# Preparing and finishing the node rows inside the edge loop of a graph attention layer

## The chip, the core and the metric

The program runs on 1 core of one Trainium2 chip. The metric is the device time of one execution in microseconds. A core has TensorE (PE in the rows, with its weight loads as PEld), VectorE (DVE), ScalarE (ACT), GpSimd (POOL) and SyncE (SP). Each works through its own list of instructions in order, and they meet at semaphores. Copies between HBM and the memory on the core go through 16 DMA engines; they are issued by SP or ACT, or, for the gathers with an index per row, by GpSimd.

## What is computed

```python
h = jnp.maximum(_layernorm(x, axis=-1), 0.0)      # x: 6250 nodes x 256
eq = h @ Wq + bq
ek = h @ Wk + bk
e = edge_attr @ We + be                            # 106250 edges x 256
m = jax.nn.relu(eq[dst] + ek[src] + e)
ft = jax.ops.segment_sum(m, dst, num_segments=6250)
return x + (ft @ Wr + br)
```

The edges come sorted by dst, and there are 17 of them per node on average (each of 50000 drawn pairs both ways, and one loop per node).

## The kernel before

Every float32 product is made of three float32r products: each operand is split into a rounded part (hi, made by ScalarE) and the rest (lo, made by VectorE), and hi·hi, hi·lo and lo·hi are added up in PSUM (`split_product`, the matmuls of line 934, whichever product it is).

**Node phase.** Nodes lie in 52 blocks of 128. SP loads x into the space that later holds `ft` (four loads), VectorE takes row statistics (line 688), GpSimd works out variance, scale and shift in three parts (lines 441 to 459). Then per block: ScalarE makes h (`make_h`, line 534), TensorE transposes it (943), ScalarE and VectorE split the transpose (541, 709), TensorE makes k and q side by side (6 matmuls of 512 columns), VectorE adds the biases from PSUM into `kq` (717), ScalarE rounds q (547), GpSimd makes q's low part (465), and SP stores the k rows in `k_table` and both q parts in `q_table` in HBM (`store_tables`, lines 305 and 310). Side work (the windows of the groups, weights of the edges, clearing `ft`, line 733) is spread over these turns.

**Edge loop.** 208 groups of 512 edges, four to a body, so 52 bodies. A group's destinations lie in a window of 48 nodes. For group n, in this order on each engine:
- GpSimd: four gathers of 128 k rows by src (`gather`, line 494) into one of four slots, once the slot's group n-4 was added (`s_pre`).
- VectorE, one step per group: `add_rows` (838: adds the gathered rows to the edge product in PSUM; it waits until the gathers of group n+1 have been written too, `s_wrote`), `make_send` (826), `add_sum` (862: adds the sum of group n-3 to `ft`), `edge_low` (818: low part of the edges of group n+2), `message_low` (846).
- ScalarE: `copy_idx` (586), `edge_high` of n+2 (594), `message_high` (615), `make_pick` of n+2 (604, 607), `take_sum` of n-1 (622).
- TensorE: `edge_product` of n+1 (28 matmuls, lines 934 and 989: the edge product and, by a one-hot matrix, the q rows of the window), `window_sum` of n-1 (8 matmuls, 1012), `turn_part` of n-2 (2 transposes, 999). The edge product of n+1 goes into the PSUM slot of n-1, so it waits for `message_low` of n-1.
- SP: loads of edges, window indices and q windows for the group four ahead.

The order that matters for VectorE and TensorE:

```python
for u in range(UNROLL):                    # VectorE
    add_rows(it, u, last)
    make_send(it, u)
    add_sum(it, u - 3, w0)
    edge_low(it, u + 2)
    message_low(it, u)
for u in range(UNROLL):                    # TensorE
    edge_product(it, u + 1)
    window_sum(it, u - 1)
    turn_part(it, u - 2)
```

**Output phase.** After the last sum, per block of `ft`: ScalarE and VectorE split it (655, 896), TensorE makes the product with Wr (6 matmuls), VectorE adds x+br, which GpSimd has prepared (512), two blocks at a time (908), and SP stores four blocks at a time (399).

All edges are done in one pass if every group's destinations fit into 48 nodes; otherwise the program repeats the loop over all windows (`more_passes`, `passes_of`).

Of the kernel before, what the change touches and what calls it, by code (L numbers as in the profile page):

```python
# [22 lines left out]
LANES = 128  # L23
NODES = 6250
# [22 lines left out]
TURNS = BLOCKS // NRING  # L47
NORM_STEPS = (None, 0, 17)
STATS_STEPS = NORM_STEPS[2]
SIDE_TURNS = 6  # L50
PAIRS = NRING // 2
X_SLOTS = 8
OUT_SLOTS = 4
LOAD_TURNS = SIDE_TURNS + UNROLL
LEAD = 2
assert TURNS % OUT_SLOTS == 1 and OUT_SLOTS == TILES and UNROLL == OUT_SLOTS and X_SLOTS == UNROLL + 4
assert BLOCKS % NRING == 0 and BLOCKS % 2 == 0 and 2 * NRING * (TURNS - SIDE_TURNS) >= BLOCKS and BLOCKS % XPARTS == 0
# [3 lines left out]
def gnn_program(nc, x, dst_groups, dst_lanes, src_lanes, edges, Wq, bq, Wk, bk, We, be, Wr, br, out):  # L61
# [5 lines left out]
    k_table = nc.dram_tensor("k_table", (ROWS, D), F32, kind="Internal").ap()  # L67
    q_table = nc.dram_tensor("q_table", (2, ROWS, D), F32R, kind="Internal").ap()
# [9 lines left out]
    with ctx:  # L78
# [12 lines left out]
        lane_raw = sb("lane_raw", [2 * WIN, PASSES], F32)  # L91
        lane_wrap = sb("lane_wrap", [2 * WIN, 1], F32)
        lane_node = sb("lane_node", [2 * WIN, PASSES], F32)
        lane_id = sb("lane_id", [2 * WIN, 1], F32)
# [9 lines left out]
        span = sb("span", [LANES, 1], F32)  # L104
        narrow = sb("narrow", [LANES, 1], F32)
# [11 lines left out]
        bias = sb("bias", [LANES, 2 * D], F32)  # L117
        bias_e = sb("bias_e", [LANES, D], F32)
        bias_r = sb("bias_r", [LANES, D], F32)
# [22 lines left out]
        gap = sb("gap", [2 * WIN, GROUP], I16)  # L142
# [7 lines left out]
        x_slots = [edge[:, u].rearrange("p h e -> p (h e)") for u in range(UNROLL)]  # L150
        slot_cols = 2 * NRING * D
        x_slots += [window_cols[:, u * slot_cols:(u + 1) * slot_cols].bitcast(F32) for u in range(3)]
        x_slots += [pre[:, 0, :]]
        x_slots = [slot.rearrange("p (b d) -> p b d", d=D) for slot in x_slots]
        result = k_rows

        kq = k_rows[:, 0:2].rearrange("p s t d -> p (s t d)").rearrange("p (b n) -> p b n", n=2 * D)
# [7 lines left out]
        sum_rows = sb("sum_rows", [LANES, 2, D], F32)  # L165

# [74 lines left out]
        def stored(eng, stores, b, u):  # L241

            if isinstance(b, int) and b < NRING:
                return
            eng.wait_ge(stores[u], 16 // NRING * (b - u))
# [850 lines left out]
```

## Time and profile before

| | us |
|---|---|
| median of 3 runs | 1247.06 (1246.17 to 1247.19) |
| the profiled execution's own time | 1248.51 |
| its span in the profile | 1246.6 |
| TensorE busy | 1119.9 (90%) |
| VectorE busy | 962.8 (77%) |
| ScalarE busy | 857.2 (69%) |
| GpSimd busy | 887.7 (71%) |
| DMA | 303.48 MB, mean 243 GB/s |

The span runs from the first to the last instruction in the profile. Busy time counts the instructions that compute (and GpSimd's writing of gather descriptors). Matmuls overlap in the array, so a busy TensorE need not be a full one. "Idle before" is the time for which an engine stood still before instructions of a group, and the name behind the arrow is what it was released by.

### The profile page before, as it was taken

The numbers are of one execution on the slowest core, as the hardware profiler recorded it, in microseconds if no ns is written. First come the engines' busy times: TensorE is split into PE (matmuls) and PEld (weight loads), VectorE is DVE, ScalarE is ACT, GpSimd is POOL, SyncE is SP. The second block draws the span as 40 slices with busy tenths as digits, with TensorE's granted clock in tenths as the row PEclk, the third lists the DMA queues.
The fourth block names the chain that finished last, engine by engine and source line by source line (L and its number), as shares of the span: only waits on it lengthen the run. The fifth ranks groups of instructions, "written<-read, shape, count | busy, mean of one in ns | idle before, by whom it ended". The sixth has DMA issues, their size and how long they took to land.

```text
span 1246.6 us, 33342 instructions
## 1 busy us (share of the span) xinstructions
PE 1119.9 (90%) x8632; PEld 1051.0 (84%) x8632; DVE 962.8 (77%) x1324; ACT 857.2 (69%) x1463; POOL 887.7 (71%) x946
## 2 busy tenths in 40 slices
PE   1997799999999999999999999999999999999876
PEld 1775789889898888898898988888988989898875
DVE  5887577777777777777777777777777777777798
ACT  1676577777777777777777777777777777777542
POOL 4454777777777777777777777777777777777644
PEclk9999999999999999999999999999999999999989
DMA  8888777777778777777777777777877787877664
GB/s 249 273 275 273 237 244 246 245 244 243 254 246 248 245 246 247 250 248 244 244 245 251 244 252 245 244 247 247 251 246 245 245 248 242 256 244 244 209 191 140
DMA packets 164469, 303.48 MB, mean 243 GB/s; under 512 B 29204, under 2 KB 110740, under 8 KB 164452
## 3 DMA queue, kind: packets, MB, share of 16 engines
q1 hardware_dynamic: 124516, 194.18, 50.0%
q0 software_dynamic: 39936, 109.11, 27.0%
q8 instruction: 6, 0.10, 0.0%
q14 instruction: 11, 0.09, 0.0%
HBM read 275.69 MB, written 27.48 MB: 243 GB/s over the span
## 4 chain that ended last, share of the span: by engine, by line
POOL 46%; issue 37%; PE 9%; DVE 3%; DMA 3%; ACT 1%; POOLq 1%; SPq 0%; DVEq 0%; ACTq 0%
POOL k_rows L494 46%; PE p_sum L934 5%; PE p_edge L934 3%; DVE hT_lo L896 1%; DMA ft<-in_x 1%; PE p_turn L943 1%; DMA k_rows<-k_table,idx 1%; POOLq L502 0%; DMA pre<-in_dst_groups 0%; DMA range_table<-top_g 0%; DVE k_rows L908 0%; DVE k_rows L717 0%; POOLq L492 0%; DVE p_edge L838 0%; ACT hT_hi L655 0%
## 5 line engine op out<-in xcount | busy, mean ns | idle before, releaser
L494 POOL DMA_INDIRECT k_rows<-k_table,idx x832 | 799.3, 961 | 255.9 <-issue 255.0
L934 PE MATMUL p_edge<-we_hi,edge_hi 128*128 128x256 f32 x1664 | 487.0, 293 | 75.9 <-DVE m_lo L846 67.1
L934 PE MATMUL p_edge<-we_lo,edge_hi 128*128 128x256 f32 x1664 | 465.4, 280 | 0.0
L934 PE MATMUL p_edge<-we_hi,edge_lo 128*128 128x256 f32 x1664 | 465.1, 280 | 0.0
L838 DVE TENSOR_TENSOR p_edge<-p_edge,k_rows 128x1024 f32<-128x1024 f32 x208 | 256.4, 1233 | 244.7 <-DMA k_rows<-k_table,idx 244.6
L934 PEld LDWEIGHTS p_edge<-we_hi,edge_hi 128*128 128x128 f32 x1664 | 314.4, 189 | 122.2 <-issue 66.9
L615 ACT ACTIVATE m_hi<-p_edge 128x1024 fp32r<-128x1024 f32 x208 | 213.8, 1028 | 262.2 <-DVE p_edge L838 262.2
L934 PEld LDWEIGHTS p_edge<-we_lo,edge_hi 128*128 128x128 f32 x1664 | 315.1, 189 | 0.0
L934 PEld LDWEIGHTS p_edge<-we_hi,edge_lo 128*128 128x128 f32 x1664 | 313.2, 188 | 0.0
L818 DVE TENSOR_TENSOR edge_lo<-edge,edge_hi 128x1024 fp32r<-128x1024 f32 x208 | 253.6, 1220 | 0.9 <-ACT edge_hi L594 0.9
L846 DVE SCALAR_TENSOR_TENSOR m_lo<-p_edge,m_hi 128x1024 fp32r<-128x1024 f32 x208 | 253.2, 1217 | 1.3 <-ACT m_hi L615 1.3
L989 PE MATMUL p_edge<-q_win,pick 96*128 96x256 f32 x832 | 236.3, 284 | 0.0
L594 ACT ACTIVATE edge_hi<-edge 128x1024 fp32r<-128x1024 f32 x208 | 220.3, 1060 | 4.9 <-PE p_edge L989 4.9
L1012 PE MATMUL p_sum<-m_hi,send 128*128 128x256 f32 x832 | 208.1, 283 | 0.3 <-ACT sum_rows L622 0.3
L1012 PE MATMUL p_sum<-m_lo,send 128*128 128x256 f32 x832 | 207.9, 282 | 0.0
L1012 PEld LDWEIGHTS p_sum<-m_hi,send 128*128 128x128 f32 x832 | 157.1, 189 | 0.6 <-issue 0.6
L1012 PEld LDWEIGHTS p_sum<-m_lo,send 128*128 128x128 f32 x832 | 156.9, 189 | 0.0
L989 PEld LDWEIGHTS p_edge<-q_win,pick 96*128 96x128 f32 x832 | 156.3, 188 | 0.0
L604 ACT ACTIVATE gap<-rel_row,lane_node 96x512 int16<-96x512 int16 x208 | 147.4, 709 | 2.8 <-DMA rel_row<-rel_table 2.7
L607 ACT ACTIVATE pick<-gap 96x512 fp32r<-96x512 int16 x208 | 131.5, 632 | 6.6
L622 ACT ACTIVATE sum_rows<-p_sum 128x256 f32<-128x256 f32 x208 | 78.7, 378 | 10.1 <-PE p_sum L1012 4.0
L999 PE MATMUL p_turn<-ident,sum_rows 128*128 128x128 f32 x416 | 79.9, 274 | 2.3 <-DVE ft L862 1.8
(81 smaller groups left out, 937.8 us busy)
## 6 DMA issues: line engine op xcount, KB each, us to landing
edge<-in_edges SPq DMA_DIRECT2D x208, 512.0 KB, 4.0
rel_row<-rel_table SPq DMA_DIRECT2D x208, 96.0 KB
q_win<-q_table SPq DMA_DIRECT2D x416, 48.0 KB
q_table<-m_hi SPq DMA_DIRECT2D x52, 256.0 KB, 2.6
k_rows<-k_table,idx POOLq DMA_INDIRECT x832
ft<-in_x SPq DMA_DIRECT2D x4, 1664.0 KB, 12.7
k_table<-k_rows SPq DMA_DIRECT2D x52, 128.0 KB, 2.9
out_rows<-k_rows SPq DMA_DIRECT2D x13, 512.0 KB, 3.1
```

The lines of the kernel that those rows point to most:

```text
L494: nc.gpsimd.indirect_dma_start(out=k_rows[:, slot, j, :], out_offset=None, in_=k_table, in_offset=bass.IndirectOffsetOnAxis(ap=idx[:, slot ...
L594: nc.scalar.activation(edge_hi[:, slot % 2], edge[:, slot], ACT.Copy).then_inc(s_ehi, 1)
L604: nc.scalar.activation(gap[:], rel_row[:, slot, :], ACT.Abs, scale=-1.0, bias=lane_node[:, bass.ds(ps, 1)]).then_inc(s_gap, 1)
L607: nc.scalar.activation(pick[:, slot % 2, :], gap[:], ACT.Relu, bias=1.0, scale=-1.0)\
L615: nc.scalar.activation(m_hi[:, slot % 2, :], p_edge[:, slot % 2, :], ACT.Relu).then_inc(s_mhi, 1)
L818: nc.vector.tensor_tensor(edge_lo[:, slot % 2], edge[:, slot], edge_hi[:, slot % 2].bitcast(F32), ALU.subtract).then_inc(s_elo, 1)
L838: nc.vector.tensor_tensor(p_edge[:, slot % 2, :], p_edge[:, slot % 2, :], k_rows[:, slot].rearrange("p t d -> p (t d)"), ALU.add).then_inc ...
L846: nc.vector.scalar_tensor_tensor(m_lo[:, slot % 2, :], p_edge[:, slot % 2, :], 0.0, m_hi[:, slot % 2, :].bitcast(F32), ALU.max, ALU.subtract)\
L934: ins = nc.tensor.matmul(target, a(h), b[:, h, :], start=(h == 0 and n == 0), stop=(stop and h == HALVES - 1 and n == 2))
L989: ins = nc.tensor.matmul(target, pick[:, slot % 2, tile], q_win[:, slot, :], start=False, stop=True)
L999: ins = nc.tensor.transpose(p_turn[:, 0, h * LANES:(h + 1) * LANES], sum_rows[:, slot % 2, h * LANES:(h + 1) * LANES], ident[:])
L1012: ins = nc.tensor.matmul(p_sum[:, 0, 0:D], send[:, slot % 2, j, :], m[:, slot % 2, j * D:(j + 1) * D], start=(j == 0 and m is m_hi), stop= ...
```

## The change

- The node phase makes only k, for 50 blocks in 25 pairs, fully unrolled: h of two blocks, four transposes, one split of both, 12 matmuls of 256 columns, one copy from PSUM (by ScalarE for even pairs, by VectorE for odd ones, no bias), one store of two blocks. The k bias goes into q's. q is made there only for the first four blocks. All x loads are issued first, the weights come over ScalarE's queue, and the norm has four parts, the first of 8 blocks. GpSimd makes no q part any more and clears `ft` in five pieces.
- Bodies 0 to 45 of the edge loop each make one more block of q, at body plus four: SP loads its x again; ScalarE makes h (`next_h`) in step 0; TensorE transposes it in step 0; both parts are split in step 1; TensorE makes q in step 2 with 8 matmuls (two of them add the bias by a row of ones); ScalarE and VectorE split q in step 3 (`next_q_high`, `next_q_low`); SP stores it two bodies later in its own order.
- Every body makes one block of output, six blocks behind (`out_block`; the first six bodies write blocks that are written again at the end): `ft_high` and `ft_low` in step 2, 8 matmuls (`emit`) in step 3, and `finish` on VectorE after `message_low` of step 3, which adds x from an SP load; SP stores it.
- Behind the loop stand three blocks (46 to 48), with VectorE adding x itself. GpSimd's x+br is gone.
- The window check also asks that the windows go in order: `in_order` is true if every window start lies at most 208 nodes ahead and 512 behind 128 times its body.

```diff
-XPARTS = 4
-XPART = BLOCKS // XPARTS
-NORM_STARTS = (0, BLOCKS // 4, BLOCKS // 2, BLOCKS)
+NODE_BLOCKS = 50
+NODE_PAIRS = NODE_BLOCKS // 2
+NORM_STARTS = (0, 8, 20, 34, NODE_BLOCKS)
 NORM_PARTS = len(NORM_STARTS) - 1
...
+FIRST_Q = NRING
+Q_BODIES = NODE_BLOCKS - FIRST_Q
...
+OUT_LAG = 6
+OUT_BODIES = BODIES - OUT_LAG
+TAIL = tuple(range(OUT_BODIES, -(-NODES // LANES)))
+OUT_SPAN = (OUT_LAG - 2) * LANES
...
+            for v in range(NODE_PAIRS):
+                store_k(v)
+                if v in (2, 3):
+                    store_first_q(v - 2)
...
+                if v in range(8, 8 + 2 * UNROLL, 2):
+                    load_edge(0, (v - 8) // 2)
...
+            def load_next_x(it):
+
+                source = one_block(x_blocks, it + FIRST_Q)
+                after(sp, s_hq, it - 1)
+                sp.dma_start(xq, source).then_inc(s_xq, 16)
...
+                after(sp, s_qnhi, it)
+                after(sp, s_qnlo, it)
+                sp.dma_start(target.bitcast(F32), q_next.bitcast(F32)).then_inc(s_qnext, 16)
...
+            def load_out_x(it):
+
+                source = one_block(x_blocks, out_block(it))
+                after(sp, s_fin, it - 1)
+                sp.dma_start(out_x[:, 0, :], source).then_inc(s_xo, 16)
...
+            def store_out(it):
+
+                target = one_block(out_blocks, out_block(it))
+                after(sp, s_fin, it)
+                sp.dma_start(target, result[:, 0, :]).then_inc(s_out, 16)
+
+            def loads(it):
+                if not isinstance(it, int):
+                    sp.wait_ge(s_qnext, (it - 2) * 16)
+                elif it > 2:
+                    sp.wait_ge(s_qnext, (min(it, Q_BODIES + 2) - 2) * 16)
                 for u in range(UNROLL):
                     load_edge(it, u)
                     load_row(it, u)
                     load_window(it, u)
...
+                    if u == 2:
+                        if not isinstance(it, int) or it > 1:
+                            store_out(it - 2)
+                        load_out_x(it - 1)
+                    if u == 3 and (not isinstance(it, int) or it > 1):
+                        store_next_q(it - 2)
+                    if u == 3 and (not isinstance(it, int) or it < Q_BODIES):
+                        load_next_x(it)
...
+            sp.wait_ge(s_qnext, Q_BODIES * 16)
+            with sp.Fori(Q_BODIES + 2, bodies) as it:
+                later_loads(it)
+            store_out(bodies - 2)
+            load_out_x(bodies - 1)
+            store_out(bodies - 1)
+            sp.wait_ge(s_out, bodies * 16)
+            sp.sem_inc(s_go_sp, 1)
+            for t, b in enumerate(TAIL):
+                sp.wait_ge(s_fin, bodies + t + 1)
...
+            for part in range(NORM_PARTS):
+                variance(part)
+                scale_and_shift(part)
+            for c in range(CLEARS):
+
+                cleared = slice(c * NODE_BLOCKS // CLEARS, (c + 1) * NODE_BLOCKS // CLEARS if c < CLEARS - 1 else BLOCKS)
+                pool.wait_ge(s_hn, (c + 1) * NODE_BLOCKS // CLEARS)
+                nc.gpsimd.memset(x_all[:, cleared, :], 0.0).then_inc(s_cleared, 1)
...
-            pool.wait_ge(s_pre, bodies * UNROLL)
-            for t in range(TURNS):
-
-                pool.wait_ge(s_xo[t % X_SLOTS], 16 * (t // X_SLOTS + 1))
-                after(pool, s_free, t - OUT_SLOTS)
-                nc.gpsimd.tensor_tensor(result[:, t % OUT_SLOTS], x_slots[t % X_SLOTS],
-                                        bias_r[:].unsqueeze(1).to_broadcast([LANES, NRING, D]),
-                                        ALU.add).then_inc(s_xbr, 1)
...
+            for v in range(NODE_PAIRS):
+                if v + 1 < NODE_PAIRS:
+                    make_h(2 * v + 2)
+                    make_h(2 * v + 3)
+                h_hi(v)
+                if v > 0 and v % 2 == 1:
+                    copy_k(v - 1)
+                if v in (1, 2):
+                    first_q_high(v - 1)
...
+            def ft_high(it):
+
+                block_cols = bass.ds(out_block(it) * LANES, LANES)
+                after(act, s_ft, it * UNROLL - 2)
+                after(act, s_outp, it - 1)
+                nc.scalar.activation(hT_hi[:, 0, :].rearrange("p (h n) -> p h n", h=HALVES),
+                                     ft[:, :, block_cols], ACT.Copy).then_inc(s_fhi, 1)
+
+            def next_h(it):
+
+                act.wait_ge(s_xq, (it + 1) * 16)
+                act.sem_inc(s_go_act, 1)
+                nc.scalar.activation(hq, xq, ACT.Relu, bias=shift[:, bass.ds(it + FIRST_Q, 1)],
+                                     scale=rstd[:, bass.ds(it + FIRST_Q, 1)]).then_inc(s_hq, 1)
...
+            def next_h_high(it):
+
+                after(act, s_hqT, it)
+                after(act, s_qnp, it - 1)
+                nc.scalar.activation(hT_hi[:, 1, :], p_next, ACT.Copy).then_inc(s_hqhi, 1)
+
+            def next_q_high(it):
+
+                after(act, s_qnp, it)
+                if not (isinstance(it, int) and it == 0):
+                    act.wait_ge(s_qnext, it * 16)
+                nc.scalar.activation(q_next[:, 0, :], p_next, ACT.Copy).then_inc(s_qnhi, 1)
...
+                    if u == 0 and q:
+                        next_h(it)
+                    if u == 1 and q:
+                        next_h_high(it)
+                    if u == 2:
+                        ft_high(it)
+                    if u == 3 and q:
+                        next_q_high(it)
...
+            dve.wait_ge(s_const, 7)
+            for v in range(NODE_PAIRS):
+                h_lo(v)
+                for b in range(ready, min(ready + STATS_PER_PAIR, NODE_BLOCKS)):
+                    row_statistics(b)
+                ready += STATS_PER_PAIR
+                if v > 0 and v % 2 == 0:
+                    copy_k(v - 1)
...
+            def ft_low(it):
+                after(dve, s_ft, it * UNROLL - 1)
+                after(dve, s_fhi, it)
+                after(dve, s_outp, it - 1)
+                nc.vector.tensor_tensor(hT_lo[:, 0, :].rearrange("p (h n) -> p h n", h=HALVES),
+                                        ft[:, :, block_cols],
+                                        hT_hi[:, 0, :].bitcast(F32).rearrange("p (h n) -> p h n", h=HALVES),
+                                        ALU.subtract).then_inc(s_flo, 1)
+
+            def finish(it):
+                after(dve, s_outp, it)
+                dve.wait_ge(s_xo, (it + 1) * 16)
+                if not (isinstance(it, int) and it == 0):
+                    dve.wait_ge(s_out, it * 16)
+                nc.vector.tensor_tensor(result[:, 0, :], p_res, out_x[:, 0, :], ALU.add).then_inc(s_fin, 1)
...
+                    if u == 1 and q:
+                        next_h_low(it)
+                    if u == 2:
+                        ft_low(it)
+                    if u == 3 and q:
+                        next_q_low(it)
                     message_low(it, u)
+                    if u == 3:
+                        finish(it)
...
+            def with_bias(target, bias_hi, bias_lo, a_hi, a_lo, b_hi, b_lo):
+
+                for n, b in enumerate((bias_hi, bias_lo)):
+                    nc.tensor.matmul(target, ones[:], b[:], start=(n == 0), stop=False)
+                return split_product(target, a_hi, a_lo, b_hi, b_lo, start=False)
...
+            def k_product(v):
+
+                after(pe, s_hhi, v)
+                after(pe, s_hlo, v)
+                k_copied(pe, v - 2)
+                for i in range(2):
+                    u = (2 * v + i) % NRING
+                    ins = split_product(p_sum[:, v % 2, i * D:(i + 1) * D], turned(hT_hi, u), turned(hT_lo, u),
+                                        wk_hi, wk_lo)
+                ins.then_inc(s_kp, 1)
...
+            def turn_next_h(it):
+
+                after(pe, s_hq, it)
+                after(pe, s_qnlo, it - 1)
+                for h in range(HALVES):
+                    ins = nc.tensor.transpose(p_next[:, h * LANES:(h + 1) * LANES], hq[:, h * LANES:(h + 1) * LANES],
+                                              ident[:])
+                ins.then_inc(s_hqT, 1)
+
...
+                    if u == 0 and q:
+                        turn_next_h(it)
+                    if u == 2 and q:
+                        next_q_product(it)
+                    if u == 3:
+                        emit(it)
...
+            for t in range(len(TAIL)):
+                pe.wait_ge(s_flo, bodies + t + 1)
+                out_product(p_tail[:, t, 0:D], 1 + t).then_inc(s_outp, 1)
```

## Rows read from the trace of the kernel before

**Rows 1.** Windows: length; busy of PE, PEld, DVE, ACT, POOL; PEclk, DMA share, GB/s
```profile
0.00:30.60 30.60, 5.74 (x20) 4.08 (x20) 17.06 (x38) 5.93 (x11) 12.61 (x30) 1.00 0.86 248
30.60:121.40 90.80, 82.78 (x396) 64.81 (x396) 76.61 (x171) 62.65 (x157) 43.94 (x71) 0.98 0.84 278
...
160.00:1160.00 1000.00, 940.30 (x7535) 896.09 (x7534) 777.94 (x992) 732.88 (x1188) 758.68 (x793) 1.00 0.78 247
...
1184.50:1246.60 62.10, 42.34 (x312) 40.16 (x312) 54.61 (x78) 21.39 (x52) 26.30 (x11) 0.91 0.51 165
```

**Rows 2.** Groups by line, 160 to 1160 us: busy, mean ns | idle before, releaser
```profile
L494 POOL DMA_INDIRECT k_rows<-k_table,idx x793 | 758.9, 957 | 241.6 <-issue 241.6
...
L934 PEld LDWEIGHTS p_edge<-we_hi,edge_hi 128*128 128x128 f32 x1587 | 299.2, 189 | 103.9 <-DVE m_lo L846 54.1 <-issue 49.8
...
L838 DVE TENSOR_TENSOR p_edge<-p_edge,k_rows 128x1024 f32<-128x1024 f32 x199 | 245.3, 1233 | 223.0 <-DMA k_rows<-k_table,idx 223.0
```

**Rows 3.** Timeline, one group of the edge loop: start, length (us), instruction
```profile
603.73 1.23 DVE L838 TENSOR_TENSOR p_edge<-p_edge,k_rows 128x1024 f32<-128x1024 f32 x1 [0.98 <-DMA k_rows<-k_table,idx]
...
604.00 0.95 POOL L494 DMA_INDIRECT k_rows<-k_table,idx  x1 [0.30 <-issue]
...
605.26 0.95 POOL L494 DMA_INDIRECT k_rows<-k_table,idx  x1 [0.31 <-issue]
...
605.30 1.22 DVE L818 TENSOR_TENSOR edge_lo<-edge,edge_hi 128x1024 fp32r<-128x1024 f32 x1
...
606.44 1.22 DVE L846 SCALAR_TENSOR_TENSOR m_lo<-p_edge,m_hi 128x1024 fp32r<-128x1024 f32 x1
...
606.52 0.95 POOL L494 DMA_INDIRECT k_rows<-k_table,idx  x1 [0.30 <-issue]
...
607.80 0.35 PE L934 MATMUL p_edge<-we_hi,edge_hi 128*128 128x256 f32 x1 [0.21 <-DVE m_lo L846]
```

**Rows 4.** Timeline, the third group of the loop
```profile
144.88 1.22 DVE L818 TENSOR_TENSOR edge_lo<-edge,edge_hi 128x1024 fp32r<-128x1024 f32 x1
...
145.01 1.92 POOL L494 DMA_INDIRECT k_rows<-k_table,idx  x1 [0.30 <-issue]
```

**Rows 5.** Timeline, the head: row statistics, h, first biased rows, first gather
```profile
10.90 4.35 DVE L688 BATCH_NORM_STATS2 stats<-ft 128x6 f32<-128x256 f32 x13
...
20.80 1.58 ACT L534 ACTIVATE hn<-ft,norm 128x256 f32<-128x256 f32 x3 [2.08 <-POOL norm L459]
...
30.64 0.67 DVE L717 TENSOR_TENSOR k_rows<-p_sum,bias 128x512 f32<-128x512 f32 x1
...
121.42 1.21 POOL L494 DMA_INDIRECT k_rows<-k_table,idx  x1 [2.71 <-issue]
```

**Rows 6.** Groups by line, 36 to 112 us, and the stores' time to landing
```profile
L717 DVE TENSOR_TENSOR k_rows<-p_sum,bias 128x512 f32<-128x512 f32 x45 | 31.1, 690 | 9.4 <-PE p_sum L934 8.1 <-POOL m_hi L465 0.9
L709 DVE TENSOR_TENSOR hT_lo<-p_turn,hT_hi 128x256 fp32r<-128x256 f32 x45 | 18.8, 418 | 1.7 <-ACT hT_hi L541 1.4 <-DVE lane_node L761 0.2
L688 DVE BATCH_NORM_STATS2 stats<-ft 128x6 f32<-128x256 f32 x19 | 7.4, 415 | 0.0
k_table<-k_rows SPq DMA_DIRECT2D x52, 128.0 KB, 2.9
```

**Rows 7.** Timeline, the end: last gather, last sum, last addition
```profile
1172.99 0.95 POOL L494 DMA_INDIRECT k_rows<-k_table,idx  x1 [0.31 <-issue]
...
1184.24 0.26 DVE L862 TENSOR_TENSOR ft<-ft,p_turn 128x96 f32 x1 [1.92 <-PE p_turn L999]
...
1242.22 0.69 DVE L908 TENSOR_TENSOR k_rows<-p_edge,k_rows 128x512 f32<-128x512 f32 x1 [0.72 <-PE p_edge L934]
```

**Rows 8.** Timeline, TensorE after it stood still for 8.85 us
```profile
125.67 0.41 PE L934 MATMUL p_edge<-we_lo,edge_hi 128*128 128x256 f32 x1
125.89 0.41 PE L934 MATMUL p_edge<-we_hi,edge_lo 128*128 128x256 f32 x1
```

**Rows 9.** Groups by line, 1180 to 1247 us
```profile
L896 DVE TENSOR_TENSOR hT_lo<-ft,hT_hi 128x256 fp32r<-128x256 f32 x52 | 40.5, 812 | 2.0 <-ACT hT_hi L655 1.9
```

More of the change, by code:

```diff
@@ L224, in gnn_program @@
         s_ft = sem("ft_added")
[L225 removed]
+        s_xo = sem("out_x_loaded")
+        s_xtail = sem("tail_x_loaded")
         s_fhi = sem("ft_hi_ready")
@@ new lines, in later_loads @@
+            def later_loads(it):
+                for u in range(UNROLL):
+                    load_edge(it, u)
+                    load_row(it, u)
+                    load_window(it, u)
+                    if u == 2:
+                        store_out(it - 2)
+                        load_out_x(it - 1)
+            for it in (1, 2):
+                loads(it)
+            with sp.Fori(3, Q_BODIES) as it:
+                loads(it)
+            for it in (Q_BODIES, Q_BODIES + 1):
+                loads(it)
@@ new lines, in first_q_high @@
+            def first_q_high(v):
+                after(act, s_qp, v)
+                nc.scalar.activation(q_parts[:, 2 * v:2 * v + 2, 0], p_first[:, v], ACT.Copy).then_inc(s_qhi, 1)
+            for b in range(2):
+                make_h(b)
+            for v in range(NODE_PAIRS):
[7 more added lines that the diff above has]
+                    first_q_high(v - 1)
@@ L578, in _ @@
-            for u in range(NRING):
-                node_step(TURNS - 1, u, last=True)
-            round_q(BLOCKS - 1, NRING - 1)
+            copy_k(NODE_PAIRS - 1)
             def copy_idx(it, u):
@@ L853, in window_of, with add_sum @@
                 return window_start(dve, w, ps)
-            def add_sum(it, u, w0):
+            def add_sum(it, u, w0, read=None, split=None):
                 _, slot, n, _, _ = visit(it, u)
                 after(dve, s_turn, n)
+                if read is not None:
+                    after(dve, s_fhi, read)
+                if split is not None:
+                    after(dve, s_flo, split)
                 after(dve, s_ft, n - 1)
@@ L901, in finish @@
-            def finish(it, j, v):
-                t = OUT_SLOTS * it + j
-                after(dve, s_outp, NRING * t + 2 * v + 1)
-                after(dve, s_xbr, t)
-                pair = result[:, j, 2 * v:2 * v + 2, :]
-                nc.vector.tensor_tensor(pair, p_out[:, j % 2, v].rearrange("p (b d) -> p b d", d=D), pair,
-                                        ALU.add).then_inc(s_fin, 1)
-            def out_turn(it, j, last=False):
-                for u in range(NRING):
-                    if not (last and u + 3 >= NRING):
-                        ft_low(NRING * (OUT_SLOTS * it + j) + u + 3, (u + 3) % NRING)
-                    if u % 2:
-                        finish(it, j, u // 2)
@@ L918, in _ @@
[L918 to L925 removed]
+            for t, b in enumerate(TAIL):
+                dve.wait_ge(s_fhi, bodies + t + 1)
+                nc.vector.tensor_tensor(hT_lo[:, 1 + t, :].rearrange("p (h n) -> p h n", h=HALVES),
+                                        ft[:, :, b * LANES:(b + 1) * LANES],
+                                        hT_hi[:, 1 + t, :].bitcast(F32).rearrange("p (h n) -> p h n", h=HALVES),
+                                        ALU.subtract).then_inc(s_flo, 1)
```

594 lines of the change are left out of this document (282 added, 312 removed).

## The prediction, made before the changed kernel ran

> **What bounds the kernel now.** I read the windows first [rows 1]: the first gather starts at 121.4 us, the edge loop runs to about 1184, and 62 us of output phase follow. The head and the output phase are what the change attacks, and the loop is where it puts the work. In the middle 1000 us TensorE is busy for 940, which looks full, but its weight loads stand still for 103.9 us [rows 2]. GpSimd issues 793 gathers in that stretch, each 957 ns of writing and 305 ns of issue that nothing external ends. So a gather costs 1.261 us, a group 5.04 and a body 20.2. VectorE idles 223.0 us, 1.12 per group, until gathers arrive. One group shows the order of events [rows 3]: GpSimd ends a gather, VectorE adds rows at 603.73, `message_low` ends at 607.66, and TensorE starts the next edge product at 607.80. TensorE's wait for VectorE is really a wait for GpSimd.
>
> TensorE's own need per group is 5.04 less its idle 103.9/198 = 0.52, so 4.52 us for 38 matmuls, 0.119 each. Its slack is 2.1 us per body.
>
> The rows hide a second clock. Counted from `add_rows`, gathers start at +0.27, +1.53 and +2.79, and `edge_low` runs from +1.57 to +2.71. It fits between two starts with 0.04 and 0.08 us to spare. In the third group, where no `add_sum` stands ahead of it, `edge_low` starts 0.13 us before a gather, and that gather takes 1.92 us: it ends 0.91 after `edge_low` does [rows 4]. Gathers that start inside `add_rows` (604.00) or `message_low` (606.52) take 0.95 as ever [rows 3]; those two read PSUM, `edge_low` reads two SBUF tiles. So a gather whose start falls under a VectorE operation on two SBUF tiles waits for its end.
>
> **Head.** Row statistics started at 10.90 behind the reductions of dst, and h at 20.80 [rows 5]. Now x comes first, 8 blocks of 1.05 MB; at 248 GB/s [rows 1] that is 4.2 us, so statistics start near 6, and five fewer of them save 5 × 0.34. That puts h at about 14.2 and, with transposes and splits, the first product at 17.6. Consecutive VectorE operations overlap by 0.08, so 512 columns cost 0.61 and a statistic 0.34 [rows 6]. The first nine pairs are VectorE's: 0.61 + 4 × 0.34 + half a copy 0.31 = 2.3 us, together 20.5, plus 4.0 for dst reductions and 1.2 for the first q. The other 16 pairs are TensorE's: 4 transposes and 12 matmuls, 1.9 us, together 30.5, plus 3 for ten linked window operations that hold up one split. Products end at 76.8. Copy 0.5, issue 0.4, landing 2.9 [rows 6] and 0.7 to the first gather, with rounding up for first-use stalls: first gather at **82**, against 121.4. Gain **39.4**, bounds 29 (h no earlier, every pair 2.1) and 46. The clears on GpSimd need only h and end under the last pair; if they did not, the last piece would hold the loop back, and that is part of the lower bound, as are weights and biases (now on ScalarE's queue, beside x) that come after the statistics, for which I allow 5 us.
>
> **End.** Before, the last gather starts at 1172.99 and ends at 1173.94, the last sum at 1184.5, the last addition ends at 1242.91, and 3.7 us of store follow [rows 7]. The 10.6 us from gather to sum stay, with 1 for the last `emit` and `finish`. Then three blocks: ScalarE's and VectorE's first split 0.9, 24 matmuls at 0.119 to 0.213 (TensorE at 1.2 GHz, the lower of its levels, after standing still [rows 8]; 2.9 to 5.1 us), an addition 0.5, a store 3.7. End 19.6 to 21.8 after the last gather, against 72.7: gain **52**, within 2. VectorE's splits took 812 ns there [rows 9] beside GpSimd's additions of x+br, which are gone.
>
> **Loop, TensorE.** A q body adds 2 + 8 + 8 = 18 matmuls and transposes, at 0.119 each 2.14 us (the bias matmuls have one row; no row shows such a one, so they cost nothing or as much as the others, and I take the latter), against 2.1 of slack. That alone makes it 20.2 or 20.3: nothing.
>
> **Loop, VectorE.** Four operations of 0.34 against 4.5 us of idle, but their places count. `ft_low` reads two SBUF tiles (`ft`, `hT_hi`) and in step 2 runs from +2.71 to +3.05, over the gather start at +2.79: **0.26** per body. The other three have a PSUM operand and block nothing.
>
> `finish` waits for `emit`, and behind it in VectorE's list is the next `add_rows`. Counted from `add_rows` of step 1: `message_low` ends at 3.93 + 0.34 = 4.27, TensorE starts 0.14 later, runs step 2 (38 + 8 matmuls, 5.47) and step 3 (5.47), the last result drains in 0.16, and `finish` takes 0.34: 15.9. GpSimd would release the next `add_rows` after three groups and the 0.26, at 15.1 + 0.26 = 15.4, or 15.55 as the loop's turn adds about 0.2. VectorE is 0.35 to 0.5 late; `edge_low` then ends that much later and covers the gather start at +2.79: **0.27 to 0.4**. I take 0.3. This lateness doesn't grow, for the blocked gather puts the two back in step.
>
> A q body costs 0.56 more, times 46 = 25.8; the six without q have only `ft_low`, 1.6. Sum **+27**. Bounds: +2 (no gather blocked) and +1.8 per body (below).
>
> The Trainium skill (SBUF — State Buffer, section "SBUF: two separate sides") says that VectorE operations with two SBUF inputs and GpSimd operations that read SBUF exclude each other, whichever began first holding the port for its whole length. The trace agrees for a gather that begins second; the other way it differs, since `edge_low` starts 0.04 us after a gather and still takes 1.22 [rows 3]. By the page a late `ft_low` or `edge_low` could wait up to 0.95 us as well, some 40 us in all, and the sum would be near 1225.
>
> **Loop, ScalarE, SP and DMA.** ScalarE is busy 73% [rows 1]; four operations of about 0.4 (as `hT_lo` of as many columns [rows 6]) make it 81%. `next_q_high` is the delicate one: it waits for the store of the q before, which SP issues only behind the window loads of this body's last edge product. That lands some 4 us after that product, while q is ready 2.3 us after it. The next `message_high` is due just then, so a store 1 us slower is late for it. SP's other waits (for the store it has just issued, about 3 us) hold up edge loads that have 15 us to spare. DMA gets 640 KB per body on top of 4.98 MB, 13%: 78% becomes 88%.
>
> **Sum.** 1246.6 − 39.4 − 52 + 27 = 1182.2 span. The profiled execution took 1248.51 for its span, and the median is 0.5 over the span, so **1183**. This case's own range is 1165 to 1200.
>
> **Rivals.**
> - *The loop hides everything.* Gathers are not blocked by `ft_low`, as they are only just not by `edge_low`. 1246.6 − 39.4 − 52 + 2 = 1157. For: VectorE idles 4.5 us per body. Against: the gather of 1.92 us [rows 4].
> - *The loop turns from GpSimd-bound to chain-bound.* TensorE's slack is used up to 0.1 us, so any wait (late q store, late x, gathers landing later at 88% DMA) adds directly. At 1.0 to 1.8 us per q body: 1201 to 1238, middle 1218. For: TensorE has no room and three queues gained a wait. Against: every one of those waits has its result early by 0.5 us or more on paper.
> - *Slower than before: gathers blocked in every group.* The margin ahead of `edge_low` is 0.04 us. If the added waits make it start under the gather, each group takes 0.97 more, as the third group's gather of 1.92 did [rows 4], and so 6.0 us. It decides once bodies exceed 20.2 + 91.4/46 = 22.2 us; with 0.97 per group throughout, 1155 + 52 × 3.9 = 1358. Against: the order ahead of `edge_low` is unchanged, and lateness only closes the other margin.
> - *It does not do what it says.* If the windows were out of order the loop would repeat 131 times. With 17 edges per node a body covers 120.5 nodes, so the start drifts to 6130 − 6528 = −398, short of −512, and never 208 ahead. Excluded.
>
> **How the numbers follow.** Forecast 0.46, everything hidden 0.16, chain-bound 0.27, slower 0.09, near no change 0.02. The range must leave out no more than 0.2: the slower case, the no-change case and the edges of two others. I give **1157 to 1228**. A measurement of this kernel can tell about 0.2% (2.5 us). Faster 0.88, same 0.02, slower 0.10, the last taking in the slowest end of the chain-bound case.
>
> **What would show it.** First gather near 82. A q body of 20.6 to 20.9 between equal `add_rows`, a plain one near 20.4. Two long gathers per q body, one under `ft_low`, one under `edge_low` of step 0, each 0.2 to 0.5 us over 0.95, and TensorE's weight loads almost without idle. After the last gather about 21 us. I am wrong if gathers keep 0.95 throughout, if VectorE waits for q or `message_low` for ScalarE, or if `add_rows` no longer follows the end of a gather.

## The result, and the profile after

The changed kernel takes 1255.77 us (1252.61 to 1257.33, 4 runs) against 1246.62 (1245.06 to 1247.19, 4 runs): a ratio of 1.0072, 95% interval 1.0049 to 1.0096. It is slower by 9 us where 64 us less was forecast, and outside the range. Its profiled span is 1250.8 us.

The page of the changed kernel, busy time and share:
```profile
span 1250.8 us, 34423 instructions
PE 1159.1 (93%) x9236; PEld 1106.5 (88%) x9236; DVE 948.6 (76%) x1366; ACT 863.1 (69%) x1542; POOL 882.4 (71%) x901
```
Its windows, with the columns of [rows 1]:
```profile
160.00:1160.00 1000.00, 963.11 (x7755) 922.93 (x7754) 781.24 (x1092) 712.26 (x1271) 748.40 (x734) 1.00 0.82 258
...
1225.20:1250.80 25.60, 19.26 (x130) 16.97 (x130) 13.58 (x25) 7.93 (x14) 0.94 (x1) 0.88 0.11 32
```
and GpSimd's first and last gather, on its timeline:
```profile
94.52 1.46 POOL L555 DMA_INDIRECT k_rows<-k_table,idx  x1 [6.25 <-issue]
...
1225.20 0.95 POOL L555 DMA_INDIRECT k_rows<-k_table,idx  x1 [0.30 <-issue]
```
These lines cut the span into three parts that can be set beside the prediction's sum (in the kernel before the first gather starts at 121.42 [rows 5], the last at 1172.99 [rows 7]):

| part | before | after | difference | predicted |
|---|---|---|---|---|
| start to first gather | 121.4 | 94.5 | −26.9 | −39.4 |
| first to last gather | 1051.6 | 1130.7 | **+79.1** | **+27** |
| last gather to the end | 73.6 | 25.6 | −48.0 | −52 |
| span | 1246.6 | 1250.8 | +4.2 | −64 |

Three quarters of the miss lie in the loop. In 1000 us GpSimd now issues 734 gathers, not 793. Groups by line, 160 to 1160 us (rows to set beside [rows 2]):
```profile
L555 POOL DMA_INDIRECT k_rows<-k_table,idx x734 | 749.9, 1022 | 251.9 <-issue 215.0 <-ACT idx L645 30.5 <-DVE p_edge L923 6.4
L923 DVE TENSOR_TENSOR p_edge<-p_edge,k_rows 128x1024 f32<-128x1024 f32 x182 | 222.7, 1224 | 42.8 <-issue 21.9 <-DMA k_rows<-k_table,idx 20.9
L970 DVE TENSOR_TENSOR pre<-p_turn,pre 128x256 f32<-128x256 f32 x46 | 19.5, 425 | 41.9 <-PE p_turn L1039 41.8
L712 ACT ACTIVATE hn<-p_sum 128x256 fp32r<-128x256 f32 x44 | 16.9, 384 | 118.3 <-DMA q_table<-hn 118.3
```
Read them in this order. A gather has gone from 957 to 1022 ns: more gathers start while a VectorE operation on two SBUF tiles holds them up ("covered" starts). VectorE's wait for gathers in `add_rows` has gone from 223.0 to 20.9 us: it is no longer early. In its place stand `finish` (L970), which waits 41.8 us for TensorE's output product, and ScalarE's `next_q_high` (L712), which waits 2.7 us in a q body for the store of the q before.

The gathers of one q body, GpSimd's timeline:
```profile
600.33 1.23 POOL L555 DMA_INDIRECT k_rows<-k_table,idx  x1 [0.30 <-issue]
...
604.38 1.36 POOL L555 DMA_INDIRECT k_rows<-k_table,idx  x1 [0.30 <-issue]
...
610.02 0.94 POOL L555 DMA_INDIRECT k_rows<-k_table,idx  x1 [0.53 <-issue]
...
612.52 1.84 POOL L555 DMA_INDIRECT k_rows<-k_table,idx  x1 [0.30 <-issue]
...
622.24 1.23 POOL L555 DMA_INDIRECT k_rows<-k_table,idx  x1 [0.30 <-issue]
```
The body is 622.24 − 600.33 = 21.91 us. The twelve left out are of 0.94 to 0.99, each with 0.30 or 0.31 before it. Sixteen plain ones at 1.2525 give 20.04; 0.28, 0.41 and 0.89 for three covered starts, 0.06 in small pieces and 0.23 of waiting make up the rest. All three start under an `edge_low` (of steps 2, 3 and 0) and end 0.80 to 0.82 us after it; none starts under `ft_low`.

GpSimd has hardly a pause, and yet the gathers no longer set the body. `add_rows` of a group waits until the gathers of the next one are written. Counted through the program, that was so 0.03 us before it started in the kernel before (0.23 at the head of a body). In the changed kernel it was so 3.0 to 6.7 us before (five q bodies from 545 us on; 2.8 to 6.2 in three plain ones). What does set the body is a chain, here in the q body from 610.75 to 632.66. VectorE's and TensorE's timelines:
```profile
610.75 1.23 DVE L923 TENSOR_TENSOR p_edge<-p_edge,k_rows 128x1024 f32<-128x1024 f32 x1 [0.92 <-issue]
...
613.45 1.22 DVE L931 SCALAR_TENSOR_TENSOR m_lo<-p_edge,m_hi 128x1024 fp32r<-128x1024 f32 x1
```
```profile
614.73 0.39 PE L1039 MATMUL p_edge<-we_hi,edge_hi 128*128 128x256 f32 x1 [0.56 <-DVE m_lo L931]
...
630.83 0.28 PE L1039 MATMUL p_turn<-wr_hi,hT_lo 128*128 128x256 f32 x1
```
```profile
631.32 0.42 DVE L970 TENSOR_TENSOR pre<-p_turn,pre 128x256 f32<-128x256 f32 x1 [1.01 <-PE p_turn L1039]
632.66 1.23 DVE L923 TENSOR_TENSOR p_edge<-p_edge,k_rows 128x1024 f32<-128x1024 f32 x1 [0.91 <-DMA k_rows<-k_table,idx]
```
From `add_rows` of step 0 to TensorE's edge product that waits for its `message_low`: 3.98 us. TensorE then runs steps 1 to 3 without standing still, to the end of the output product at 631.11: 16.38. From there over `finish` to the next `add_rows`: 1.55. The sum is 21.91, the whole body.

The last link shows best in a body without q. VectorE's timeline:
```profile
1195.00 1.22 DVE L931 SCALAR_TENSOR_TENSOR m_lo<-p_edge,m_hi 128x1024 fp32r<-128x1024 f32 x1
1198.72 0.42 DVE L970 TENSOR_TENSOR pre<-p_turn,pre 128x256 f32<-128x256 f32 x1 [2.51 <-PE p_turn L1039]
1200.34 1.23 DVE L923 TENSOR_TENSOR p_edge<-p_edge,k_rows 128x1024 f32<-128x1024 f32 x1 [1.19 <-DMA k_rows<-k_table,idx]
...
1201.91 1.22 DVE L903 TENSOR_TENSOR edge_lo<-edge,edge_hi 128x1024 fp32r<-128x1024 f32 x1
1203.05 1.22 DVE L931 SCALAR_TENSOR_TENSOR m_lo<-p_edge,m_hi 128x1024 fp32r<-128x1024 f32 x1
```
and TensorE's at the output product before it:
```profile
1196.81 0.39 PE L1119 MATMUL p_turn<-ident,sum_rows 128*128 128x128 f32 x2
1197.13 0.38 PE L1046 MATMUL p_turn<-br_hi,ones 1*128 1x256 f32 x1
1197.35 0.27 PE L1046 MATMUL p_turn<-br_lo,ones 1*128 1x256 f32 x1
1197.55 0.39 PE L1039 MATMUL p_turn<-wr_hi,hT_hi 128*128 128x256 f32 x1
1197.78 0.28 PE L1039 MATMUL p_turn<-wr_lo,hT_hi 128*128 128x256 f32 x1
1197.89 0.28 PE L1039 MATMUL p_turn<-wr_hi,hT_lo 128*128 128x256 f32 x1
```
VectorE stands still for 2.51 us in front of `finish`, which ends at 1199.14; only 1.20 us later does `add_rows` start, and the q bodies show the same kind of gap (0.92 at 610.75). The view names the gathers for it, but those that it waits for had been written by 1194.24. The chain that ended last, as the profile follows it, shows what VectorE's sequencer (DVEq) did in the gap: the loop's turn (line 1014) and the load of the next window's start into a register (line 937):
```profile
1198.86 0.06 DVEq L1014
...
1199.17 0.14 DVEq L1014
...
1199.42 0.31 DVEq L937
...
1199.76 0.19 DVEq L937
```
From 160 to 1160 us VectorE stands still in front of `add_rows` 46 times, once per body, for 42.8 us in all (line L923 above). In the kernel before, this work lay under the wait for gathers. TensorE's view holds the other surprise: the two bias matmuls of one row (`1*128`) start 0.32 us after the transposes, and the next three starts are 0.22, 0.20 and 0.23 apart, where matmuls of full height are 0.11 to 0.12 apart.

### The profile page after: what moved, and what is told of

It reads as the page before. It is cut to its first block, busy times and chain, and to the rows that moved or that the text cites. A ratio compares the mean times of both kernels' runs of the same rounds, so it can differ in the third digit from the quotient of the medians.

```text
span 1250.8 us, 34423 instructions
## 1 busy us (share of the span) xinstructions
PE 1159.1 (93%) x9236; PEld 1106.5 (88%) x9236; DVE 948.6 (76%) x1366; ACT 863.1 (69%) x1542; POOL 882.4 (71%) x901
## 3 DMA queue, kind: packets, MB, share of 16 engines
q10 hardware_dynamic: 1096, 1.05, 0.3%
## 4 chain that ended last, share of the span: by engine, by line
PE 46%; issue 17%; POOL 15%; DVE 11%; DVEq 4%; DMA 4%; ACT 2%; ACTq 0%; SPq 0%; POOLq 0%
PE p_edge L1039 24%; POOL k_rows L555 15%; PE p_sum L1132 7%; PE p_sum L1039 4%; PE p_edge L1109 4%; DVE m_lo L931 3%; DVE p_edge L923 3%; DVE edge_lo L903 2%; PE p_turn L1039 2%; DMA k_rows<-k_table,idx 2%; DVEq L937 2%; PE p_turn L1119 2%; PE p_turn L1046 1%; DVE send L911 1%; DMA q_table<-hn 1%
## 5 line engine op out<-in xcount | busy, mean ns | idle before, releaser
L555 POOL DMA_INDIRECT k_rows<-k_table,idx x832 | 850.1, 1022 | 287.7 <-issue 248.7
L1039 PE MATMUL p_edge<-we_hi,edge_hi 128*128 128x256 f32 x1664 | 479.4, 288 | 55.3 <-DVE m_lo L931 39.2
L923 DVE TENSOR_TENSOR p_edge<-p_edge,k_rows 128x1024 f32<-128x1024 f32 x208 | 254.6, 1224 | 64.6 <-DMA k_rows<-k_table,idx 42.0
L663 ACT ACTIVATE rel_g<-rel_row,lane_node 96x512 int16<-96x512 int16 x208 | 147.8, 711 | 1.6 <-DMA rel_row<-rel_table 1.5
L666 ACT ACTIVATE pick<-rel_g 96x512 fp32r<-96x512 int16 x208 | 131.4, 632 | 6.6
L712 ACT ACTIVATE hn<-p_sum 128x256 fp32r<-128x256 f32 x46 | 17.6, 383 | 121.5 <-DMA q_table<-hn 121.5
```

The lines of the kernel that those rows point to most:

```text
L555: nc.gpsimd.indirect_dma_start(out=k_rows[:, slot, j, :], out_offset=None, in_=k_table, in_offset=bass.IndirectOffsetOnAxis(ap=idx[:, slot ...
L663: nc.scalar.activation(gap[:], rel_row[:, slot, :], ACT.Abs, scale=-1.0, bias=lane_node[:, bass.ds(ps, 1)]).then_inc(s_gap, 1)
L666: nc.scalar.activation(pick[:, slot % 2, :], gap[:], ACT.Relu, bias=1.0, scale=-1.0)\
L923: nc.vector.tensor_tensor(p_edge[:, slot % 2, :], p_edge[:, slot % 2, :], k_rows[:, slot].rearrange("p t d -> p (t d)"), ALU.add).then_inc ...
L1039: ins = nc.tensor.matmul(target, a(h), b[:, h, :], start=(start and h == 0 and n == 0), stop=(stop and h == HALVES - 1 and n == 2))
```

## The experiments

Two theories stood against each other. **A**: a chain through TensorE's output product, `finish` and the next `add_rows` sets the body, with the q store as a second wait. **B**: shared resources set it (more blocked gathers, more DMA, a full TensorE). The kernel before was timed on the same chip as each run; it took 1246.7 to 1247.7 us but for the runs told of last.

**Finish one body later.** Body 1 is written out, and one more `finish` follows the last body.
```diff
-                    if u == 3:
-                        finish(it)
+                    if u == 0 and not first:
+                        finish(it - 1)
```


> VectorE's `finish` is moved behind `message_low` of step 0 of the next body, where its output product is long done. Theory A (the loop is bound by a chain: emit, finish, turn of VectorE's loop, add_rows, message_low, edge product): VectorE's idle of 2.5 us before `finish` and TensorE's idle of 1.3 us in the same body go, a body without q falls from 21.4 to 20.5 us, one with q from 21.9 to 21.3, and the span from 1251 to about 1215. Theory B (the loop is bound by GpSimd's blocked gathers and by TensorE's longer list, not by who waits for whom): at most 0.2 us per body, 1240 or more.

**The q store two steps earlier** in SP's list.
```diff
-                    if u == 3 and (not isinstance(it, int) or it > 1):
+                    if u == 1 and (not isinstance(it, int) or it > 1):
                         store_next_q(it - 2)
```


> SP stores the q block of two bodies ago behind the window loads of its second group, not of its fourth, so that ScalarE's `next_q_high` finds it landed. Theory A: ScalarE's idle before it (2.7 us per body) goes, q bodies come down to the 21.4 us of the plain ones, which keep theirs, so 46 x 0.5 = 23 us: about 1228. Theory B: ScalarE had time to spare, and nothing changes by more than 5 us: 1246 to 1251.

**Both.**


> Both moves. Theory A: all bodies are bound by GpSimd or TensorE alone; TensorE's list with its one-row matmuls comes to 20.8 us in a q body, so 20.9 there and 20.5 in the others, 1195 to 1200 in all. Theory B: the two together give under 15 us, 1236 or more.

Measured: 1217.12 us (ratio 0.9757, 0.9722 to 0.9792), 1255.5 (1.007, 1.0056 to 1.0084) and 1197.61 (0.9601, 0.957 to 0.9631). The first and the last rest on two runs each. The chain is real: without it the kernel takes 38 us less. In the profiled executions 29.4 of 34.6 us lie between the first and the last gather (1101.3 in place of 1130.7), and VectorE waits for gathers again (49.7 us in 77 waits from 200 to 900 us). Theory A was wrong on the early store alone: it expected 1228 us, and nothing changed, as B had it. The store's wait lies beside the chain, not on it. It is a second wait of the kind that shows only once the first is gone: nothing alone, 20 us on top of the other. The waits from 200 to 900 us show where it went (us in total, times, longest). In the kernel with the early store alone:
```profile
DVE pre L970 <- PE p_turn L1039: 93.6, 31, 3.0
ACT hn L712 <- PE p_sum L1039: 6.4, 32, 0.2
```
ScalarE's wait has vanished, and VectorE waits 3.0 us in front of `finish` instead. With both edits, the windows:
```profile
200.00:900.00 700.00, 700.00 (x5723) 679.44 (x5723) 582.33 (x809) 540.78 (x944) 535.81 (x540) 1.00 0.88 271
```
TensorE is busy for 700.00 of 700 us, with a body of 20.79. Only here is TensorE the bound, as B had it, and its list is 0.57 longer than my 20.22 (four groups of 4.52 and 2.14). `add_rows` follows the written gathers by 0.03 us here too; that TensorE is the one that decides shows in the next two runs.

**Bias matmuls left out** (both edits in; q and the output lack their biases), and **bias matmuls over all 128 rows**: same count, same sums. The four bias tiles (`bq_hi`, `bq_lo`, `br_hi`, `br_lo`) get 128 rows, cleared by GpSimd, with the values in row 0.
```diff
-        bq_hi = sb("bq_hi", [1, D], F32R)
+        bq_hi = sb("bq_hi", [LANES, D], F32R)
...
-        ones = sb("ones", [1, LANES], F32R)
+        ones = sb("ones", [LANES, LANES], F32R)
```


> The kernel with both edits (finish one body later, the q store two steps earlier), with the two one-row matmuls that add the bias left out of every output and q product, so q and the output are without their biases. If TensorE's list is now the bound (20.79 us per body with no idle time) and a one-row matmul costs 0.2 us rather than the 0.12 of a full one: four fewer per q body take 0.6 to 0.8 us off each of 48 q bodies and 0.3 to 0.4 off each of the 6 others, 30 to 40 us, unless the gathers (19.9 to 20.2 us per body of 20) take over as the bound, which leaves 20 to 30: 1168 to 1178 us. If one-row matmuls cost as much as the others: 0.24 to 0.48 us per body, 1178 to 1186 us. If not TensorE but the chain sets the body: 1197 us as before.

> The kernel with both edits, and the bias matmuls over all 128 rows: the bias tiles have their values in row 0 and zeros below, the stationary operand is 128 by 128 of ones. Same number of matmuls, same sums. If it is the change of height between one row and 128 that costs (cadence 0.20 to 0.23 where others have 0.119): four of them per q body at 0.119 take 0.3 to 0.6 us off a q body, 15 to 25 us in all, 1172 to 1183 us. If a one-row matmul is slow for another reason (its accumulation start, a new bank) or TensorE is not the bound: 1197 us within 3.

Measured: 1170.3 us (0.9395, 0.9374 to 0.9415) and 1173.18 (0.9409, 0.9387 to 0.9431), against 1197.61. Leaving the four matmuls out gives 27 us; giving them 128 times as many rows gives 24 of those. The work was never the cost, the change of height was. TensorE's timeline with full height:
```profile
613.25 0.39 PE L1126 MATMUL p_turn<-ident,sum_rows 128*128 128x128 f32 x2
613.39 0.36 PE L1053 MATMUL p_turn<-br_hi,ones 128*128 128x256 f32 x1
613.59 0.28 PE L1053 MATMUL p_turn<-br_lo,ones 128*128 128x256 f32 x1
613.71 0.28 PE L1046 MATMUL p_turn<-wr_hi,hT_hi 128*128 128x256 f32 x1
613.83 0.28 PE L1046 MATMUL p_turn<-wr_lo,hT_hi 128*128 128x256 f32 x1
```
From the first transpose to the second wr matmul it is 613.83 − 613.25 = 0.58 us; with one-row matmuls 1197.78 − 1196.81 = 0.97. So a product costs 0.39 less, a q body's list 0.78. Between the two bias matmuls themselves hardly anything changes (0.20, with one row 0.22): 0.18 of the 0.39 lies in front of them and 0.19 behind, where the height changes. The body itself fell by 0.5, to 20.3, for there the gathers take over again (20.04 and one blocked start of 0.22). Without any bias matmuls it is 20.3 as well. The blocked gather there starts 0.07 us into `ft_low` and takes 1.17.

**Full-height bias alone**, in the changed kernel.


> Full-height bias matmuls alone, a third time, since both chips of the last runs paused in every body (kernel before 1593 and 1611 us). Where the kernel before takes about 1247 us: theory A (the finish chain sets every body, and the output product's 0.26 to 0.3 us are on it) 1226 to 1242 us; theory B (TensorE has idle time in the changed kernel) 1256 us.

Measured: 1217.62 us (0.9753, 0.9736 to 0.9771), 38 us less than the changed kernel and below both numbers named. A q body is 21.15 us, a plain one 21.0. The wait for TensorE in front of `finish` went from 27.3 to 1.7 us between 200 and 900 us:
```profile
DVE pre L975 <- PE p_turn L1044: 1.7, 6, 0.6
ACT hn L716 <- DMA q_table<-hn: 94.5, 33, 3.9
```
A plain body has one such product and lost 21.38 − 21.0 = 0.38, a q body has two and lost 21.91 − 21.15 = 0.76. That is the 0.39 of each, where theory A had 0.26 to 0.3. How well it agrees may be luck: in this kernel `finish` hardly waits any more, and in steps 1 to 3 `add_rows` follows the written gathers again, by 0.03 to 0.24 us. This one edit, which touches no order and no wait, turns the change from 0.7% slower to 2.5% faster.

**Is a covered start the price of a blocked gather?** In the kernel before, one more VectorE operation of 256 columns behind `edge_low` in step 2; its result is not read. Once with two SBUF operands, once with one of them in PSUM.
```diff
                         edge_low(it, u + 2)
+                    if u == 2:
+                        nc.vector.tensor_tensor(hT_lo[:, 0, :], hT_hi[:, 1, :].bitcast(F32), hT_hi[:, 0, :].bitcast(F32), ALU.subtract)
```
The other has `p_sum[:, 1, 0:D]` as its first operand.

> The kernel before, with one more VectorE operation per body (256 columns, both operands and the output in SBUF, behind edge_low in step 2, where the next gathers are due; its result is never read). Theory G (such an operation holds up the start of the gather that falls on it): in the kernel before the gathers set the pace, so a body grows by about the 0.26 us that ft_low took beyond its gather, 52 bodies give 13.5 us, in all about 1260 us (at least 1255), and VectorE's own list has room for the operation. Theory H (gathers are not touched by it, VectorE waits for them anyway): 1247 us, within 2 us.

> The same extra VectorE operation in the kernel before, in the same place, but its first operand is read from PSUM in place of SBUF. Theory G (only operations with both operands in SBUF hold up a gather): 1247 us, within 2 us. If any VectorE time behind edge_low is what costs: the same as with the operands in SBUF, 1255 to 1260 us.

Measured: 1258.37 us (1.0101, 1.008 to 1.0123) and 1246.75 (0.9999, 0.999 to 1.0009). Both operations take 0.42 us; only the one with two SBUF operands costs, 11.6 us, 0.22 per body. Its place on VectorE's timeline, and the gather on GpSimd's:
```profile
615.38 0.41 DVE L875 TENSOR_TENSOR hT_lo<-hT_hi 128x256 fp32r<-128x256 f32 x1
```
```profile
615.46 1.16 POOL L494 DMA_INDIRECT k_rows<-k_table,idx  x1 [0.30 <-issue]
```
The gather due 0.08 us into it takes 0.21 longer. With one operand in PSUM it is due 0.08 us into it as well and keeps its 0.95:
```profile
609.52 0.42 DVE L875 TENSOR_TENSOR hT_lo<-p_sum,hT_hi 128x256 fp32r<-128x256 f32 x1
```
```profile
609.60 0.95 POOL L494 DMA_INDIRECT k_rows<-k_table,idx  x1 [0.30 <-issue]
```
This shows the one term of my loop sum that rested on a row of the third group [rows 4].

**The head.** ScalarE's copy of an even pair's k rows, one pair later.
```diff
-                if v > 0 and v % 2 == 1:
-                    copy_k(v - 1)
+                if v > 1 and v % 2 == 0:
+                    copy_k(v - 2)
```


> The changed kernel with ScalarE's copy of the k rows of an even pair one node pair later, so that the next rows of h are not queued behind a product that has only just begun. Theory A: the waits of 1 to 2.9 us in front of that copy and VectorE's 2.4 us behind it go, two pairs take 3.8 to 4.2 us rather than 4.58, the first gather comes 4 to 8 us earlier, 1248 to 1252 us in all (the loop behind it starts earlier and is otherwise the same). Rival: the head is paced by another list (TensorE at its low clock, VectorE), first gather at 94 to 95 us, 1256 us.

**All four edits.**


> All four edits, a third time. Where the kernel before takes about 1247 us: 1168 to 1170 us, since the first gather came 4.3 to 5.5 us earlier in the kernels with the later copy on both of those chips (89.2 and 89.5 against 93.8 to 94.8 us), and the first three edits gave 1173.2 us; 1173 us if the loop gives it back.

In the changed kernel two pairs took 4.57 us. ScalarE's timeline there:
```profile
71.71 0.58 ACT L607 ACTIVATE hT_hi<-p_turn 128x512 fp32r<-128x512 f32 x1
73.35 0.60 ACT L613 ACTIVATE k_rows<-p_sum 128x512 f32<-128x512 f32 x1 [1.05 <-PE p_sum L1039]
73.84 1.08 ACT L598 ACTIVATE hn<-ft,norm 128x256 f32<-128x256 f32 x2
...
77.92 0.60 ACT L613 ACTIVATE k_rows<-p_sum 128x512 f32<-128x512 f32 x1 [1.05 <-PE p_sum L1039]
```
The copy waits 1.05 us for a product that TensorE has only begun, with the next h behind it. With all four edits, the same copies (line 617 there) come without a wait, and two pairs take 3.71:
```profile
73.72 0.59 ACT L617 ACTIVATE k_rows<-p_sum 128x512 f32<-128x512 f32 x1
...
77.43 0.59 ACT L617 ACTIVATE k_rows<-p_sum 128x512 f32<-128x512 f32 x1
```
All four give **1169.12 us, ratio 0.9375 (0.9362 to 0.9388)**, the best version, 6% under the kernel before; the first gather starts at 87.6 us, against 94.6 with three edits. Of these 7 us only 4 reach the end (1173.18 to 1169.12, measured on two chips). The edit alone ran only on one of the chips below: its first gather started at 94.9 us there, no earlier than without it (94.5). With all four edits it came at 89.5 and 89.2 on two of those chips, against 93.3 to 94.8 in the kernels without this edit. Among kernels with the same head it moves from 92.0 to 96.9 us, so the head's gain is shown in three pairs of four, and its size only roughly.

**Left open.** Nine runs fell on three chips on which every kernel, the one before too (1593 to 1611 us), took much longer: 6.7 to 7 us per body in the kernel before. They were four of these kernels, three of them once more, and the two below. Their times say little of the kernel elsewhere. Against the kernel before on the same chip: full-height bias alone 0.9692 and 0.9737; with finish one body later 0.9553, 0.9588 and 0.9531; all four 0.9506 and 0.9567; the later copy alone 0.9676. The last two, full-height bias with finish one body later (its third time) and with the early store:

> Finish one body later and full-height bias matmuls, the q store where the change has it. Full-height bias alone gave 1217.6 us with 21.15 us per q body, and finish one body later alone 1217.1 us with 21.2. In both ScalarE waits about 3 us per q body for the q store. If that wait sets the q body in both, together they stay at 21.1 to 21.2 there and gain only in the bodies without q: 1210 to 1217 us. If TensorE's list decides: 1193 us or less.

> The q store earlier and full-height bias matmuls, finish where the change has it. The early store alone gave nothing (1255.5 us), because VectorE's wait for the output product took its place. If full-height products end that wait (1.7 us of it were left in 700 us with them, against 27.3), the q body falls from 21.15 to TensorE's 20.3 to 20.6 and all comes to 1185 to 1200 us. If VectorE's wait comes back with the early store as it did without them: 1212 to 1218 us.

They gave 0.9531 (0.9485 to 0.9577) and 0.9616 (0.9563 to 0.9669). Neither of their absolute forecasts can be judged, so which wait sets a body when the bias and only one of the other two are mended stays open. All that bears on it is that both lie below full-height bias alone (0.9692 and 0.9737, on two other such chips).

## Why the prediction was wrong

- **"VectorE is 0.35 to 0.5 late … This lateness doesn't grow": the step that failed.** I let GpSimd's gathers set the body and VectorE trail them. The trace has the chain above setting it, with the gathers written 3.0 to 6.7 us ahead. By my own terms the chain comes to 3.93 + 0.14 to the edge product, 130 matmuls at 0.119 = 15.47, and 0.16 + 0.34 + 0.2 for the drain, `finish` and the loop's turn: 20.24, less than the 20.74 that I had for the gathers. It is 21.91. Of the 1.67 more, 0.91 lie in TensorE's list, 0.78 of them the change of height, and 0.85 behind the output product (1.55 in place of 0.7); the stretch up to the edge product was 0.09 shorter.
- **The loop's turn.** In a plain body I had `finish` end 0.50 us after TensorE's last output matmul (which ends at 1198.51) and `add_rows` follow at once, or 0.2 later. The trace has 1198.72 − 1198.51 = 0.21 of waiting for the result, 0.42 for `finish`, and 1.20 to `add_rows`: 1.83 in place of 0.5 to 0.7. I had charged the turn 0.2 and the register load nothing. Both were hidden under `add_rows`'s wait for gathers [rows 2], and a wait put in front of them takes that cover away. It was also wrong that the blocked gather "puts the two back in step": the gathers stay ahead in spite of three blocked ones per q body.
- **Blocked gathers: the mechanism is right, the place and the size were not.** Two were forecast, 0.26 under `ft_low` and 0.3 under step 0's `edge_low`; three came, 0.28, 0.41 and 0.89, all under an `edge_low`. That 0.28 is so near 0.26 is luck: the gather began 0.34 us before `ft_low`. With both edits and full-height bias one does begin in `ft_low`, and costs 0.22. In the changed kernel none of this is on the chain.
- **The bias matmuls "cost nothing or as much as the others".** They cost 0.39 more per product. The sum had 2.14 us of work against 2.1 of slack, so a q body's 0.78 came on top in full. Cured alone, the kernel lands at 1217.6, inside my range. My two ends for an operation that no row showed were both on the cheap side.
- **The q store, "delicate", was called in time.** I had it land some 4 us after the last edge product. In the body from 600 us that product ended at 600.88, the store was issued at 602.14 and `next_q_high` started at 606.30: 5.4 us, past the 1 us of room that I gave it. This costs nothing while the chain over `finish` is longer, and 20 us once it isn't.
- **Chain-bound, the rival at 0.27, is what happened**, at 1.7 us per q body, inside its 1.0 to 1.8. But the waits that I named for it (late q store, late x, late gathers) are not the one that did it. By its rule that is 1155 + 46 × 1.7 = 1233; the head's 12.5 and the end's 4 us that did not come put it over the kernel before. The slower rival (blocked in every group) did not occur.
- **Head.** The gain of 26.9 is below my lower bound of 29. h started at 16.85, not 14.2, and late pairs took 2.29 us, not 1.9. I had checked VectorE's and TensorE's lists but not what stood behind ScalarE's copy; how much of the 12.5 us that explains is open.
- **End.** 25.6 us against about 21; last sum 1241.78 − 1225.20 = 16.6 after the start of the last gather, where 11.5 had been before, as VectorE and TensorE ran behind the gathers.
- **A slip.** The excluded rival's drift is 51 × 120.5 − 6528 = −382, not −398; it excludes the case all the same.

## What to carry to other kernels

When an operation with a wait is put at the end of a loop body, charge everything that stood there under another wait: the loop's turn, register loads, the way back to the engine that it waits for. Add up the whole loop through the two engines, as a rival of its own; here it was 20.2 on paper against 20.7, and 21.9 on the chip. An engine that is never idle need not be the one that sets the pace: ask how long ahead of its use its work is done. Try a bias row padded with zeros to full height before mixing one-row matmuls into full-height ones. And mend waits in pairs: one wait alone (here the store) can be worth nothing and be worth 20 us behind the next.

## What was not expected of the hardware

- A pair of one-row matmuls between full-height ones costs 0.39 us more than a pair of 128 rows with the same result, and padding it in 98 products gave 24 to 38 us.
- A VectorE operation of 0.42 us that covers the start of a gather makes it 0.21 us longer if both operands lie in SBUF, and not at all if one lies in PSUM.
- The same programs took 1.28 to 1.32 times as long on three other chips, with instructions of unchanged length (`add_rows` 1228 ns) and pauses in front of them that the profile mostly puts down to `remote`; the head, which has no loop, ran at its usual pace (first gather at 89.2 to 94.9 us). The waits of the kernel with all four edits there, 200 to 900 us:
```profile
ACT sum_rows L685 <- remote: 223.7, 56, 6.1
DVE p_edge L928 <- remote: 104.4, 32, 4.6
```
What stops the engines there was not looked into.
